# Attention by four heads at a time, with a second set of scores that has keys on partitions

## What is computed

```
x = x + attn0(cond(x, side, ...))        # 16 heads of 16, causal, with biases
x = x + ffn0(cond2(x, side, ...))        # one fp8-quantised product
x = x + attn1(cond(x, side, ...))        # 16 heads of 16, causal, no biases
x = x + moe(cond2(x, side, ...))         # 32 experts, top 6, and a shared one
# attention, per batch and head:
scores = q @ k.T / sqrt(16);  scores[key > query] = -inf
out    = softmax(scores) @ v             # then all heads @ Wo (+ bo)
# cond: sigmoid(x) times a ratio of two decayed sums over tokens, forward and backward
```

## Time and profile before

| | us |
|---|---|
| runs of the kernel | 722.6, 727.12, 727.58 (median 727.12) |
| the profiled execution | 721.55 |
| its span | 719.6 |

### The profile page before, as it was taken

The page is one execution under the profiler, slowest core; times in us unless marked ns, Lnnn a source line. Parts: engine busy times, 40 slices in busy tenths (PEclk is TensorE's granted clock), DMA queues, the critical chain, the costliest instruction groups (busy, mean ns, idle before and its releaser), DMA issues.

```text
span 719.6 us, 10950 instructions
## 1 busy us (share of the span) xinstructions
PE 550.8 (77%) x3284; PEld 409.7 (57%) x3284; DVE 443.2 (62%) x913; ACT 345.4 (48%) x1005; POOL 437.5 (61%) x448
## 2 busy tenths in 40 slices
PE   0348898898862788879797559808999999999960
PEld 0225555555441455546454435508999999999950
DVE  3736697897898286977777582305655665555610
ACT  4146575765853575847676411103444444444430
POOL 1106486875862274857678057750777777777772
PEclk9987898989975879998999859958999999999995
DMA  8999600000000000000000323235797778878523
GB/s 297 246 223 237 171 1 1 1 0 0 1 1 0 0 1 1 1 2 0 0 0 1 121 95 119 108 117 186 191 233 208 178 195 202 217 196 214 123 27 64
DMA packets 56707, 71.61 MB, mean 100 GB/s; under 512 B 11906, under 2 KB 45037, under 8 KB 56545
## 3 DMA queue, kind: packets, MB, share of 16 engines
q1 hardware_dynamic: 40272, 57.32, 28.3%
q0 software_dynamic: 16400, 13.87, 10.4%
HBM read 42.06 MB, written 37.04 MB: 110 GB/s over the span
## 4 chain that ended last, share of the span: by engine, by line
PE 51%; DVE 17%; ACT 11%; issue 9%; POOL 7%; DMA 2%; POOLq 0%; DVEq 0%; ACTq 0%; SPq 0%
PE S L904 14%; PE PJ L917 7%; POOL xe_rows L402 6%; PE S L712 6%; PE PJ L656 5%; PE OB L743 5%; DVE negmax L1098 4%; PE TB L727 4%; PE OB L917 4%; ACT prob L491 3%; PE TB L889 3%; ACT probT L499 2%; PE S L715 2%; DVE both L989 2%; DVE fwd L977 2%
## 5 line engine op out<-in xcount | busy, mean ns | idle before, releaser
L354 POOL TENSOR_SCALAR prob<-prob,rtotal 128x128 f32<-128x128 f32 (+1 forms) x256 | 186.1, 742 | 111.9 <-DVE rtotal L1104 91.3
L491 ACT ACTIVATE prob<-S,negmax 128x128 f32<-128x128 f32 (+1 forms) x256 | 103.9, 419 | 74.7 <-DVE negmax L1098 74.6
L904 PE MATMUL S<-xgT,wgu_s 128*128 128x384 f32 x576 | 109.6, 343 | 1.2 <-DVE hidden_f L1342 1.2
L1098 DVE TENSOR_REDUCE negmax<-S 128x2 f32<-128x256 f32 (+1 forms) x128 | 64.7, 546 | 74.0 <-PE S L715 73.9
L413 POOL DMA_INDIRECT out<-sig,y_token x48 | 77.3, 1610 | 46.6 <-ACT sig L630 33.6
L904 PEld LDWEIGHTS S<-xgT,wgu_s 128*128 128x128 f32 x576 | 100.4, 190 | 1.5 <-issue 1.4
L743 PE MATMUL OB<-probT,v_sb 128*32 128x256 f32 (+1 forms) x512 | 59.9, 359 | 42.2 <-ACT probT L499 42.1
L413 POOL DMA_INDIRECT odd_out<-sig,y_token x48 | 76.7, 1598 | 23.9 <-ACT sig L630 12.6
L712 PE MATMUL S<-k_sb,q_sb 32*128 32x128 f32 (+1 forms) x512 | 82.6, 401 | 7.6 <-ACT k_sb L516 7.6
L402 POOL DMA_INDIRECT xe_rows<-x_tok,slot_i x48 | 47.2, 984 | 38.4 <-ACT x_tok L595 24.1
L727 PE MATMUL TB<-ident,prob 128*128 128x128 f32 x384 | 61.5, 302 | 11.4 <-POOL prob L354 11.3
(11 more groups left out here) (161 smaller groups left out, 921.3 us busy)
## 6 DMA issues: line engine op xcount, KB each, us to landing
xe_rows<-x8m SPq DMA_DIRECT2D x4, 3468.0 KB, 40.7
ratio<-xe_rows SPq DMA_DIRECT2D x32, 433.5 KB, 4.2
ratio<-in_wgu SPq DMA_DIRECT2D x32, 384.0 KB, 4.8
x8m<-in_wd SPq DMA_DIRECT2D x32, 256.0 KB, 2.9
x<-in_x SPq DMA_DIRECT2D x1, 1024.0 KB, 6.4
odd_out<-x8m SPq DMA_DIRECT2D x1, 1024.0 KB, 28.0
out<-side SPq DMA_DIRECT2D x8, 128.0 KB, 5.6
out<-odd_out POOLq DMA_DIRECT2D x1, 1024.0 KB, 8.0
```

Of the source, the lines that this page charges most:

```text
L354: ins = eng.tensor_scalar(p, p, rtotal[:, j % RING, st, h:h + 1], 1.0, ALU.mult, ALU.mult)
L491: ins = eng.activation(prob[:, j % RING, h, cols], S[:, 2 * (j % 2) + h, cols], ACT.Exp, bias=negmax[:, j % RING, st, h:h + 1], accum_out= ...
L904: ins = eng.matmul(S[:, m, 0:CAP], fast(wgu_s[:, j % 2, a, k, m * P:(m + 1) * P]), fast(xgT[:, j % 2, b, k, :]), start=n == 0, stop=n == N ...
L1098: ins = eng.tensor_reduce(negmax[:, j % RING, st, :], S[:, 2 * (j % 2):2 * (j % 2) + 2, cols], AX.X, ALU.max, negate=True)
```

## The change

The attention is written anew around groups of four heads (a quad, v = 0 to 15, four to a batch, u = 0 to 3), with all four banks of `S` to a quad.

- `scores(v)` as before, for four heads, only for the maxima; the mask now goes first, one product of 384 columns per head. `maxima(v)` writes the negated maxima to every 32nd column of `negmax`.
- `neg_mm(v)` turns them with two products with the identity, `neg_out(v)` (ACT) copies them to `neg_rows`. `turned_scores(v)` computes the scores again with keys on partitions, in the same four banks, and adds the maxima through products with `pick`.
- `exps(v)` is one exp of 128x1536 without sums. `select(v)` (POOL) zeroes the masked part of the two diagonal blocks with `affine_select`. There are no transposes and no copy of them.
- `pv(v)` multiplies by `v_sb` into `OB` and by ones into `TB`, which gives the sums. Per half batch `totals_inverse` (ACT) takes ln and exp of the sums, `scale_o` (DVE) refines the inverse and scales `OB`, `o_out` (ACT) copies out.
- `q_out` moves from DVE to ACT. `cst`, `q_sb`, `k_sb` and `v_sb` become double; `S`, `TB`, `PJ` and `OB` have one buffer each.
- The orders of all engines are new, and all four batches are written out. On DVE `residual(b-1)` comes last in quad u = 3; on PE `y_mm(b-1)` is in u = 2 and `v_mm(b+1)` in u = 3, ahead of `turned_scores`. All `condition`s come after the last residual.
- POOL clears more at the start; the experts' `wgu` lies over `ek` and not over `ratio`, `hs` has a buffer of its own.

The diff in its core (removed lines are left out, they are those of the functions above; in the order POOL, ACT, PE, DVE):

```diff
+            def select(L, v):
+                eng.wait_ge(sem(f"exp_{L}"), v + 1)
                 settle(eng, "pool")
+                for lo in (0, 2 * P):
+                    diag = prob[:, v % 2, :, lo:lo + P]
+                    ins = eng.affine_select(diag, diag, pattern=[[0, HPT], [1, P]], compare_op=ALU.is_ge, fill=0.0,
+                                            base=0, channel_multiplier=-1)
+                ins.then_inc(sem(f"select_{L}"), 1)
...
+                for b in range(B):
+                    for u in range(QUADS):
+                        ratio_now = ratio_of(L, b, u)
+                        if ratio_now:
+                            i, bb, n, buf = ratio_now
+                            if u % 2 == 0:
                                 bonus(bb, n, buf)
+                            else:
                                 numerator(n, buf)
+                        select(L, b * QUADS + u)
...
+            def exps(L, v):
+                eng.wait_ge(sem(f"turned_score_{L}"), v + 1)
+                if v >= 2:
+                    eng.wait_ge(sem(f"pv_{L}"), v - 1)
+                eng.activation(prob[:, v % 2, :, :], S[:, :, 0:3 * P], ACT.Exp).then_inc(sem(f"exp_{L}"), 1)
+            def neg_out(L, v):
+                eng.wait_ge(sem(f"neg_mm_{L}"), v + 1)
+                if v >= 2:
+                    eng.wait_ge(sem(f"turned_score_{L}"), v - 1)
+                eng.activation(neg_rows[:, v % 2, :], TB[:, 0, 0:T], ACT.Copy).then_inc(sem(f"neg_out_{L}"), 1)
+            def totals_inverse(L, b, c):
+                eng.wait_ge(sem(f"pv_{L}"), b * QUADS + 2 * c + 2)
+                eng.activation(den_o[:, 0, :], TB[:, 1, 0:T], ACT.Ln).then_inc(sem("total_ln"), 1)
+                eng.wait_ge(sem("total_ln"), NC * (B * L + b) + c + 1)
+                eng.activation(den_o[:, 0, :], den_o[:, 0, :], ACT.Exp, scale=-1.0).then_inc(sem("total_inv"), 1)
+            def o_out(L, b, c):
+                eng.wait_ge(sem("o_scaled"), NC * (B * L + b) + c + 1)
+                if c == 0 and b:
                     eng.wait_ge(sem(f"y_mm_{L}"), b)
                 bias = vec[:, V_BV + c:V_BV + c + 1] if L == 0 else 0.0
+                eng.activation(o_sb[:, c, :], o_neg[:, :], ACT.Identity, bias=bias, scale=-1.0)\
                    .then_inc(sem(f"o_out_{L}"), 1)
+            def q_out(L, b):
+                eng.wait_ge(sem(f"q_mm_{L}"), b + 1)
+                eng.wait_ge(sem("bq_masked"), 1)
+                if b >= 2:
+                    eng.wait_ge(sem(f"turned_score_{L}"), QUADS * (b - 1))
+                for c in range(NC):
+                    for par in range(2):
+                        bias = bq_masked[:, c, par:par + 1] if L == 0 else 0.0
+                        ins = eng.activation(q_sb[:, b % 2, 2 * c + par, :], PJ[:, c * T:(c + 1) * T], ACT.Identity,
+                                             bias=bias, scale=vec[:, V_MASK + par:V_MASK + par + 1])
+                ins.then_inc(sem(f"q_out_{L}"), 1)
...
             def attention(L):
...
+                for b in range(B):
+                    for u in range(QUADS):
+                        v = b * QUADS + u
+                        ratio_now = ratio_of(L, b, u)
+                        if ratio_now and u % 2 == 0:
+                            i, bb, n, buf = ratio_now
+                            spread_decay(i, bb, n, buf)
+                            bonus_exp(i, bb, n, buf)
+                        if b == 0 and u == 2:
+                            q_out(L, 1)
+                        exps(L, v)
+                        if v + 1 < B * QUADS:
+                            neg_out(L, v + 1)
+                        if u == 0 and b:
+                            totals_inverse(L, b - 1, 1)
+                        if u == 2:
+                            totals_inverse(L, b, 0)
+                        if ratio_now and u % 2 == 0:
+                            inverse(n)
+                        if u == 0 and b:
+                            o_out(L, b - 1, 1)
+                        if u == 2:
+                            o_out(L, b, 0)
+                        if b == 0 and u == 2:
+                            k_out(L, 1)
+                        if 0 < b < B - 1 and u == 0:
+                            q_out(L, b + 1)
+                        if 0 < b < B - 1 and u == 1:
+                            k_out(L, b + 1)
+                        if b < B - 1 and u == 3:
+                            v_out(L, b + 1)
+                totals_inverse(L, B - 1, 1)
+                o_out(L, B - 1, 1)
+                if L == 0:
+                    for done in range(B - 1):
+                        sigmoid_x(L, done)
...
+            def v_mm(L, b):
+                eng.wait_ge(sem(f"k_out_{L}"), b + 1)
+                if b >= 2:
+                    eng.wait_ge(sem(f"x_res_{L}"), b - 1)
...
+            def y_mm(L, b):
+                eng.wait_ge(sem(f"o_out_{L}"), NC * (b + 1))
+                if b == B - 1:
+                    eng.wait_ge(sem(f"x_res_{L}"), b)
+                else:
+                    eng.wait_ge(sem(f"k_out_{L}" if b < B - 2 else f"v_out_{L}"), min(b + 3, B))
...
+            def scores(L, v):
+                b, u = v // QUADS, v % QUADS
+                if u == 0:
                     eng.wait_ge(sem(f"k_out_{L}"), b + 1)
+                if v >= 2:
                     eng.wait_ge(sem(f"exp_{L}"), v - 1)
+                for i in range(HPT):
+                    eng.matmul(S[:, i, 0:3 * P], ident_b[:, :], causal_b[:, :], start=True, stop=False)
                 for st, cols in HALVES:
+                    for i in range(HPT):
                         rows = slice(i * SLOT, (i + 1) * SLOT)
+                        ins = eng.matmul(S[:, i, cols], q_sb[rows, b % 2, u, st * P:(st + 1) * P],
+                                         k_sb[rows, b % 2, u // 2, 0:P * (st + 1)], start=False, stop=st == 1)
                 ins.then_inc(sem(f"score_{L}"), 1)
+            def turned_scores(L, v):
+                b, u = v // QUADS, v % QUADS
+                eng.wait_ge(sem(f"max_{L}"), min(v + 2, B * QUADS))
+                eng.wait_ge(sem(f"neg_out_{L}"), v + 1)
+                for kt, (q_cols, cols) in enumerate(((slice(0, T), slice(0, T)), (slice(P, T), slice(T, 3 * P)))):
+                    for i in range(HPT):
+                        rows = slice(i * SLOT, (i + 1) * SLOT)
+                        eng.matmul(S[:, i, cols], k_sb[rows, b % 2, u // 2, kt * P:(kt + 1) * P],
+                                   q_sb[rows, b % 2, u, q_cols], start=True, stop=False)
+                    for i in range(HPT):
+                        rows = slice(i * SLOT, (i + 1) * SLOT)
+                        ins = eng.matmul(S[:, i, cols], pick[rows, :], neg_rows[rows, v % 2, q_cols], start=False, stop=True)
+                ins.then_inc(sem(f"turned_score_{L}"), 1)
+            def neg_mm(L, v):
+                eng.wait_ge(sem(f"max_{L}"), v + 1)
+                if v:
+                    eng.wait_ge(sem(f"neg_out_{L}"), v)
+                for st in range(T // P):
+                    ins = eng.matmul(TB[:, 0, st * P:(st + 1) * P], negmax[:, v % 2, st, :, :].rearrange("p i s -> p (i s)"),
+                                     ident[:, :], start=True, stop=True)
+                ins.then_inc(sem(f"neg_mm_{L}"), 1)
+            def pv(L, v):
+                b, u = v // QUADS, v % QUADS
+                c, par = u // 2, u % 2
+                chunk = NC * (B * L + b) + c
+                if u == 0:
                     eng.wait_ge(sem(f"v_out_{L}"), b + 1)
+                if par == 0 and chunk:
+                    eng.wait_ge(sem("o_scaled"), chunk)
+                eng.wait_ge(sem(f"select_{L}"), v + 1)
+                for dst, w in ((OB, None), (TB[:, 1, :], ones_p)):
+                    for half, q_cols, p_cols in ((0, slice(0, T), slice(0, T)), (1, slice(P, T), slice(T, 3 * P))):
+                        for i in range(HPT):
+                            head = HEADS // NC * c + 2 * i + par
+                            lhs = ones_p[:, par, :] if w is not None else v_sb[:, b % 2, half, head, :]
+                            ins = eng.matmul(dst[i * SLOT:(i + 1) * SLOT, q_cols], lhs, prob[:, v % 2, i, p_cols],
+                                             start=half == 0 and par == 0, stop=half == 1 and par == 1)
                 ins.then_inc(sem(f"pv_{L}"), 1)
             def attention(L):
...
+                scores(L, 0)
+                v_mm(L, 0)
+                neg_mm(L, 0)
+                for b in range(B):
+                    for u in range(QUADS):
+                        v = b * QUADS + u
+                        if v + 1 < B * QUADS:
+                            scores(L, v + 1)
+                        if v:
+                            pv(L, v - 1)
+                        if b == 0 and u == 2:
+                            q_mm(L, 1)
+                        if b == 0 and u == 3:
+                            v_mm(L, 1)
```

(48 more changed lines are left out.)

338 lines of the change are left out of this document (84 added, 254 removed).

## The result

The changed kernel takes 749.79 us (median; 749.06 to 751.03), the kernel before beside it on the same chip 725.5: a ratio of 1.034, 95% interval 1.029 to 1.039. It is slower, as forecast, but by 24 us and not by the 37 that separate my 764 from the median of before. The profiled execution took 749.35 us against 721.55.

What follows compares the result with a forecast made beforehand. PE led before, no engine full; the single S's chain was to decide. Each layer's 165.0 us plus 12.2 for the clock made 177.2; +15.9 and +25.0 over both attentions gave 762.5, stated as 764; own range 742 to 785, 8-in-10 range 724 to 835.

Steps and rivals of the forecast that it cites:

- The single `S` as a chain: Attention quads: turned scores, exponentials and next scores run in series on the same four banks; a step takes 9.15 us.
- rival 3: PE's products: only two heads run side by side, not four; some 870 us; 8% chance.
- Sizes within the chain: Per quad at full clock: turned scores 2.1 us, exponentials 1.47, scores 2.0, pv 1.5, projection 1.95.
- The stalls: v_mm in u = 3 of batches 1 and 2 waits for DVE's residual: 6.9 us each, four times in all.
- Rival 1: At v_mm in u = 3: the residual is ready in time and stalls don't show; 724 us; 25% chance.
- The clock: PE in the attentions: 4.5 slow spells a layer of 6.8 us at half speed, adding 12.2 us a layer.
- My sign of 0.85 or less: Profile sign for a right forecast: PE's granted clock at 0.85 or less.
- Quad 2: Third step of each layer, with k_mm ahead of scores(4): 10.35 us.
- The start: First turned_scores at 51.6 us, 2.6 before the earlier 54.17, with a first step of 7.6 us.
- rival 2: POOL's select is slow, 2.6 us each: 840 us, or 800 at 1.9 us; 15% chance.
- The select: POOL's affine_select: 1.0 us each, two per quad, ending 0.2 us after the next scores.
- Quad 12: First step of the last batch in each attention, without a projection: 8.3 us.

Runs made afterwards that it cites:

- run 4: Changed kernel with ACT's exponentials of every quad done twice, the first time into a buffer nobody reads: 801.0 us.
- run 3: Changed kernel with 14 products nobody reads on PE ahead of v_mm's wait for the residual in batches 2 and 3: 740.6 us.
- run 7: Changed kernel with ACT writing the second half of k right behind neg_out in quad 2 of each layer's first batch: 744.0 us.
- run 11: Two tests on a later 695.6 us kernel: experts' zeros started later, 695.1 us; weight's early all-reduce dropped, its maximum sent through the later one, 690.25 us.
- run 5: Changed kernel without POOL's two affine_select per quad, part of the computation left out, pv waiting for the exponentials instead: 728.3 us.
- run 1: Changed kernel with DVE's residual in quad u = 3 moved right behind maxima(v+1), ahead of the half ratio: 722.57 us.

## Why the prediction was right

The steps of the fifteen quads, forecast at the full clock and read from the starts of L754 in the two attentions:

| step of quad | forecast | first | second |
|---|---|---|---|
| 0 | 7.6 | 15.2 | 8.6 |
| 1 | 9.15 | 9.2 | 9.4 |
| 2 | 10.35 | 15.3 | 13.9 |
| 3, 5, 7, 9 | 9.15 | 8.2, 8.3, 8.8, 8.2 | 8.4, 8.5, 8.3, 8.1 |
| 4, 8 | 10.7 | 10.4, 10.4 | 10.2, 9.9 |
| 6, 10 | 16.7 | 17.9, 18.0 | 17.3, 17.8 |
| 11 | 7.6 | 7.0 | 7.0 |
| 12, 13, 14 | 8.3, 9.15, 8.3 | 10.1, 8.7, 8.3 | 10.1, 8.7, 8.3 |

*The single `S` as a chain.* Right, and tested: 1.45 us more inside it cost 1.6 a quad on average (run 4), less where pv waited for `scale_o`. Four heads do run side by side: sixteen records for pv, half of 256 and half of 128 columns, take 0.86 us, as eight such did for two heads (0.84). That is rival 3 gone. The rule on tiles in the Trainium skill, "TensorEngine Tiling (Array Packing)", section Key Properties, agrees with this trace for four.

*Sizes within the chain.* Too high by 1.0 us in a steady quad: turned 1.65 for 2.1, scores 1.62 for 2.0, and 0.2 for a select that ended before the scores. I had added 0.2 for the landing of the last result to each; the next engine starts 0.1 after the modelled end at most. Over steps 1, 3 to 5, 7 to 9, 11, 13 and 14 the forecast is 4.9 us too high in the first attention and 5.5 in the second.

*The stalls.* Right in place, count and cause, four of them; 16.7 forecast at the full clock, 15.4 to 16.1 measured with the clock held (run 3), 17.3 to 18.0 with it. Rival 1 would have had them hidden: they weren't. With DVE's order changed the kernel is at 722.6, next to that rival's 724, but that the two are so near is chance: the rival took 38 us off 762.5, the move 27 off 749.8.

*The clock.* Counted as 4.5 spells of 6.8 us at 2.7 us each, 24 us in both attentions. There was more slow time than that: 0.88 of 178.5 us and 0.89 of 168.9 leave 43 and 37 us at 1.2 GHz, where 4.5 spells are 31. My sign of 0.85 or less did not follow from that count, which makes 0.91 of a layer's 177.2. But the spells were cheaper. One behind a stall costs 2.3 (run 3), 9.2 in all, and a tail some 2.6 (y_mm 3.4 for 1.99, pv 2.7 for 1.5): 14 us are found. The spells around the first quads are not priced, so the term was up to 10 too high.

*Quad 2, missed.* 10.35 forecast with `k_mm` ahead of the scores, 15.3 and 13.9 measured. I counted PE's product and not ACT's copy of it, which stands behind o_out: 8.5 us in all (run 7), slow clock behind the wait included.

*The start, missed twice, once in each direction.* The first `turned_scores` came at 45.7 and not at 51.6: I took the end of the weight's quantisation from before, 49.61, which there was DVE's queue and not the wait for the maximum; here it ended at 43.9. And POOL's 20.57 us of "issue" at 52.49 stands in the earlier trace rows; I read past it. It made the first step 15.2 instead of 7.6 (run 11). The two nearly cancel, and that is luck.

*The select.* One takes 0.61 us alone and 0.79 on average where I had 1.0, so rival 2 is gone; 0.61 also lies under my bound of 0.7, which came from a row that was itself slowed. The figure for data-dependent branching in the Trainium skill, "GPSIMD Engine Reference", section Elementwise — side-by-side cycle accounting, weighed as that rival's tail (5.1 us, an estimate), does not fit this instruction. But the select was costed as work of POOL alone, nearly off the chain, and that step was wrong. It costs 21 us (run 5): 6.6 at the start, the rest by slower instructions on DVE and by quads in which pv waits for it.

*Between the attentions and behind them.* +6.7 for +5.4 forecast, +0.4 for +1.7.

*Quad 12.* 8.3 forecast, 10.1 measured in both: a half ratio stands in front of `scale_o` on DVE, with L1017 at 1.24 us for 0.16 and others slowed by the select (run 5).

The 13 us between 762.5 and 749.35, term by term against the measured steps: sizes -10.4, the clock's term -24.4, and within the steps, where the clock's real share lies, quad 2 +8.4, first steps +8.6, the stalls +4.1, quads 12 +3.6, tails +3; the start -5.9, between the attentions +1.3, behind them -1.3. That the total is so near owes much to terms that cancel. The stalls do not owe anything to it: they were found where forecast, and run 1 alone takes the loss away. They are not the only thing that would: without the select, which I had nearly off the chain, the loss is gone as well (run 5). The kernel is slower because it pays for both. My own range of 742 to 785 holds the result, but the terms named for its lower end, -4 and -8, reach only to 750. Of the signs, the gaps on PE came (6.5 to 6.7 us, ended by DVE's x); quads of 9 to 10 us did not, nor a clock of 0.85.
